# A decoder kernel with a recurrence: routing of the last stage inside the recurrence's laps, norms in two groups at three stage entries

## The reference

```
x = x + _L0_attn_ref(...)   # and L0_xattn, L0_ffn (router, top 2 of 8 experts)
x = x + _L1_attn_ref(...)   # and L1_xattn, L1_ffn: top 2 of 8 routed experts, 2 shared ones
x = x + _L2_attn_ref(...)   # and L2_xattn, L2_ffn: silu, gelu, gelu, scales
x = x + _L3_attn_ref(...)   # and L3_xattn, L3_ffn
```

```
routing = _l2norm(hs.reshape(B, S, E, D));  expr = (x @ expr_w.T).reshape(B, S, E, D)
gram = einsum('bsed,bsfd->bsef', routing, routing);  diff_n = _l2norm(gram - eye)
penalty = mean(sum(diff_n ** 2))              # one number over all 800 tokens
scores = (1 - cos(expr, routing)) * (1 + penalty)
top_v, top_i = top_k(scores, 2);  mult = softmax(top_v)
out = sum over the two chosen e of mult * mlp_e(x)  +  shared mlp(x)
```

## Time and profile before

| | |
|---|---|
| median of 3 runs | 3295.4 us (3287.6 to 3300.6) |
| profiled execution, own time | 3299.5 us |
| its span, first to last instruction | 3297.7 us |
| TensorE busy | 2989.2 us, 91% |
| VectorE busy | 1466.9 us, 44% |
| ScalarE busy | 741.6 us, 22% |
| GpSimd busy | 207.6 us, 6% |
| moved by DMA | 192.77 MB, mean 58 GB/s |

### The profile page before, as it was taken

The page is one execution under the profiler, slowest core; times in us unless marked ns, Lnnn a source line. Parts: engine busy times, 40 slices in busy tenths (PEclk is TensorE's granted clock), DMA queues, the critical chain, the costliest instruction groups (busy, mean ns, idle before and its releaser), DMA issues.

```text
span 3297.7 us, 62708 instructions
## 1 busy us (share of the span) xinstructions
PE 2989.2 (91%) x25725; PEld 1712.0 (52%) x25725; DVE 1466.9 (44%) x3548; ACT 741.6 (22%) x1835; POOL 207.6 (6%) x377
## 2 busy tenths in 40 slices
PE   6878889789988999899879879999999999999487
PEld 4554456579755555455546643444444444444277
DVE  4545335311256566200574422455555555555622
ACT  2331134211122454211014311111111111111100
POOL 2001110020210000000200000000000000000012
PEclk8889989699989999899889979999999999999799
DMA  4000000259400000410000076000000000000186
GB/s 144 1 1 1 13 9 1 108 191 331 152 27 1 1 1 1 138 51 26 1 1 1 2 203 184 13 21 17 21 21 17 21 17 21 21 17 21 37 284 204
DMA packets 79206, 192.77 MB, mean 58 GB/s; under 512 B 32664, under 2 KB 54917, under 8 KB 67366
## 3 DMA queue, kind: packets, MB, share of 16 engines
q1 hardware_dynamic: 74966, 184.17, 17.2%
q0 software_dynamic: 4096, 6.57, 0.7%
HBM read 161.29 MB, written 29.39 MB: 58 GB/s over the span
## 4 chain that ended last, share of the span: by engine, by line
PE 81%; DVE 9%; ACT 3%; issue 3%; DMA 2%; POOL 1%; SPq 1%; POOLq 0%; DVEq 0%; ACTq 0%
PE banks L1159 31%; PE banks L984 8%; PE banks L816 4%; PE banks L539 3%; PE banks L1127 3%; PE banks L710 3%; PE banks L492 3%; PE banks L1187 2%; PE banks L1048 2%; PE banks L1060 2%; PE banks L838 2%; PE banks L856 1%; PE banks L862 1%; PE banks L878 1%; PE banks L605 1%
## 5 line engine op out<-in xcount | busy, mean ns | idle before, releaser
L1159 PE MATMUL banks<-arena 128*32 128x384 f32 x12800 | 1032.2, 486 | 1.1 <-DVE arena L2089 1.1
L1159 PEld LDWEIGHTS banks<-arena 128*32 128x32 f32 x12800 | 431.9, 110 | 601.6 <-issue 599.2
L1498 ACT ACTIVATE arena<-arena 128x256 f32<-128x256 f32 x200 | 83.2, 416 | 753.9 <-DVE arena L2101 753.9
L2101 DVE TENSOR_TENSOR arena<-banks,arena 128x256 f32<-128x256 f32 x200 | 85.0, 425 | 293.2 <-PE banks L1159 293.2
L984 PE MATMUL banks<-arena 128*128 128x400 f32 x512 | 172.5, 499 | 1.5 <-DVE arena L2051 0.8
L816 PE MATMUL banks<-arena 128*100 128x256 f32 x512 | 150.7, 453 | 18.0 <-ACT arena L1423 5.4
L539 PE MATMUL banks<-XNT,arena 128*128 128x400 f32 x384 | 147.6, 526 | 8.3 <-ACT XNT L1251 3.9
L1240 ACT ACTIVATE arena<-banks 128x512 f32<-128x512 f32 (+2 forms) x120 | 68.6, 572 | 383.7 <-PE banks L1048 151.1
L710 PEld LDWEIGHTS banks<-arena 32*121 32x121 f32 x1536 | 105.9, 197 | 62.9 <-ACT arena L1342 47.3
L984 PEld LDWEIGHTS banks<-arena 128*128 128x128 f32 x512 | 97.1, 190 | 76.8 <-DVE arena L2051 1.4
L1698 DVE TENSOR_REDUCE arena<-banks 100x4 f32<-100x1444 f32 x64 | 106.3, 1661 | 65.0 <-PE banks L666 64.8
(11 more groups left out here) (314 smaller groups left out, 4098.6 us busy)
## 6 DMA issues: line engine op xcount, KB each, us to landing
arena<-fc SPq DMA_DIRECT2D x22, 1024.0 KB, 6.9
arena<-pj SPq DMA_DIRECT2D x22, 1024.0 KB, 5.2
arena<-gu SPq DMA_DIRECT2D x21, 1024.0 KB, 7.1
arena<-whh SPq DMA_DIRECT2D x32, 384.0 KB, 11.8
arena<-dn SPq DMA_DIRECT2D x21, 512.0 KB, 5.2
arena<-xw SPq DMA_DIRECT2D x408, 24.0 KB
xw<-arena SPq DMA_DIRECT2D x6, 1536.0 KB, 7.8
arena<-hh SPq DMA_DIRECT2D x16, 512.0 KB, 3.3
```

Of the source, the lines that this page charges most:

```text
L1159: last = nc.tensor.matmul(banks[32 * j:32 * j + 32, 2 * c + i, 0:384].rearrange("p (g n) -> p g n", g=3), hT[:, 1 - i, 32 * ub:32 * ub + 3 ...
L1498: nc.scalar.activation(rz[:, c, :], pre[:, c, :], ACT.Sigmoid).then_inc(sem["rz_done"], 1)
L2101: nc.vector.tensor_tensor(pre[:, c, :].rearrange("p (g n) -> p g n", g=2), banks[:, 2 * c + i, 0:2 * P].rearrange("p (g n) -> p g n", g=2) ...
```

## The change

Three things. First, at the three entries: batches 0 to 3 go through `statistics`, `norm_group` and a further `turn_group` inside the stream, three items before its end (`next_at`); at the entry VectorE norms batches 4 to 7 only (`norm_rest`) and TensorE transposes these (`turn_rest`). In A and B features of the first half of the tokens stand before `turn_rest`; in A the shared expert's weights are loaded before the stage ends, into another place, and `sort_pairs` comes after 8 of the 16 feature units as before, but with the router between them. `wih` moves to another place and is loaded during B's feed forward.

Second, the routing of the last stage: each lap ranks the tokens of the lap before it on VectorE (norms, scores without the penalty's factor, which doesn't change their order, two choices, places), TensorE adds two small matmuls per lap (`rank_lap`), and GpSimd scatters the lap's tokens with their pair number to `region_rows` (8 regions of 896 rows, filled beforehand from zeros with one transfer of 7.4 MB in B). TensorE's loop gets nine laps of ten steps written out. After the recurrence only the last lap is ranked, between the shared expert's features; the penalty is worked out between the tiles (`penalty`) and multiplies the stored top values.

Third, each tile's result is scattered from GpSimd straight to `pair_vals` by pair number, behind the landing of the previous one; half of the shared down product comes before the last tile's down product; eight plain loads replace the 16 gathers.

```diff
@@ TensorE, entries
-            turn_all()
-            pe.wait_ge(sem["l_rb"], 32)
-            router_rows(cent[:, :].rearrange("p (k e) -> p k e", k=C))
...
-            features(up_w[1], range(8))
+            features(up_w[1], range(0, 8, 2))
+            turn_rest("A")
+            pe.wait_ge(sem["l_rb"], 32)
+            router_rows(cent[:, :].rearrange("p (k e) -> p k e", k=C))
+            features(up_w[1], range(1, 8, 2))
             sort_pairs(0)
...
-            turn_all()
-            pe.wait_ge(sem["l_w2"], 48)
-            for f in range(8):
-                for half in range(2):
+            pe.wait_ge(sem["l_w2"], 32)
+            for q, (f, half) in enumerate(TWO_HALVES):
+                if q == 2:
+                    turn_rest("B")
...
@@ TensorE, recurrence
+            def rank_lap(lap, bank):
+
+                pe.wait_ge(sem["picked"], lap + 1)
+                chosen_l = work_l[:, 11, 0, :]
+                nc.tensor.matmul(banks[0:ROWS, bank, 0:E], earlier_l, chosen_l, start=True, stop=True, skip_group_check=True)
+                nc.tensor.matmul(banks[0:ROWS, bank, E:2 * E], ones[0:ROWS, 0:ROWS], chosen_l, start=True, stop=True, skip_group_check=True
+                                 ).then_inc(sem["ranked"], 1)
...
-            with pe.Fori(0, S // 2) as t:
+            with pe.Fori(0, LAP // 2) as t:
                 for i in range(2):
...
+                    step_of(i, 4 * t + 2 * i)
+            with pe.Fori(1, LAPS) as lap:
+                for k in range(LAP):
+                    step_of(k % 2, 2 * LAP * lap + 2 * k)
+                    if k == 6:
+                        rank_lap(lap, 4)
...
+                if t == 11:
+                    penalty_sum()
+                if t == PAIR_TILES:
+                    pe.wait_ge(sem["l_held"], 16)
+                    held_rows(range(4))
                 if t >= 1:
                     gated_down(t - 1, ups[t - 1])
-            pe.wait_ge(sem["l_held"], 16)
-            down(h3, held_down, 4, of=lambda b: slice(b, T, B))
+            held_rows(range(4, B))
@@ VectorE
+            def norm_rest(ph):
+
+                ready = norms_before(ph, len(KINDS[ph]), 0) + 1
+                inverse_root(rstd[:, 4:B], stats[:, 4:B, 7], rstd[:, B + 4:])
+                for b in range(4, B):
+                    last = nc.vector.tensor_scalar(XN[:, b * D:(b + 1) * D], X[:, b * D:(b + 1) * D], stats[:, b, 6:7],
...
                     if k == 0:
-                        dve.wait_ge(sem["l_expr"], 16 * lap)
+                        dve.wait_ge(sem["l_seen"], 16 * lap)
+                        dots_of(1, chunk, 0)
                     if k == 1:
...
+                        dots_of(2, chunk, 1)
+                    if k == 2:
+                        settle()
+                        norms_of(chunk)
+                    if k == 3:
+                        scores_of(chunk)
+                        dots_of(8, chunk, 0)
+                    if k == 4:
+                        top_of(chunk, 0)
+                        dots_of(7, chunk, 1)
+                    if k == 5:
+                        top_of(chunk, 1)
+                        lap_chosen()
+                        dots_of(6, chunk, 0)
+                    if k == 6:
+                        dots_of(3, chunk, 1)
+                        dots_of(9, chunk, 0)
+                    if k == 7:
+                        lap_placed(lap, 4)
+                        pair_products(3, 1)
...
+            gated_features(0)
+            settle()
+            norms_of(last_lap)
+            gated_features(1)
+            scores_of(last_lap)
...
@@ GpSimd
-            scatter(1)
-            gather(1)
+            norm_group("C", 2, 0)
+            pool.wait_ge(sem["l_fill"], 16)
+            for lap in range(1, LAPS + 1):
+                pool.wait_ge(sem["placed"], lap + 1)
+                pool.wait_ge(sem["l_src"], 32 * lap)
+                for k in range(2):
+                    nc.gpsimd.indirect_dma_start(region_rows[:, :], bass.IndirectOffsetOnAxis(ap=rows_il[:, k:k + 1], axis=0),
+                                                 row_src[:, k, :], None).then_inc(sem["l_sorted"], 16)
+            for t in range(PAIR_TILES):
+                pool.wait_ge(sem["y_ready"], PAIR_TILES + t + 1)
+                if t >= 1:
+                    pool.wait_ge(sem["l_pv%d" % ((t - 1) % 2)], rows_of(0, t - 1, 2))
+                nc.gpsimd.indirect_dma_start(pair_vals[:, :], bass.IndirectOffsetOnAxis(ap=sorted_ids[:, t % 5], axis=0),
+                                             pair_y[:, t % 2], None).then_inc(sem["l_pv%d" % (t % 2)], 16)
@@ SP
+            def load_sorted(t):
+
+                if t >= 5:
+                    sp.wait_ge(sem["xt_full"], PAIR_TILES + t - 4)
+                    sp.wait_ge(sem["l_pv%d" % ((t - 5) % 2)], rows_of(0, t - 5, 2))
...
+            load(arena[:, AT_WIH:AT_WIH + 6144], "wih", "l_gru")
             sp.wait_ge(sem["phase"], 4)
-            load(arena[:, 24576:30720], "wih", "l_gru")
...
+                    if k == 2:
+                        load_sources(bass.ds(lap - 1, 1), lap)
...
-            tile_transfers(1, PAIR_TILES - 1)
+            load_sources(slice(LAPS - 1, LAPS), LAPS)
+            region_transfers()
```

More of the change, by code:

```diff
@@ L98 @@
 PAIR_TILES = (T * 2 + E * (P - 1)) // P
+TWO_HALVES = [(0, 0), (1, 0), (0, 1), (1, 1)] + [(f, half) for f in range(2, 8) for half in range(2)]
 class Count:
@@ L1216, in _, with held_rows @@
             ups = []
+            def held_rows(batches):
+                for b in batches:
+                    tokens("d", [(h3[:, f, b:T:B], held_down[:, f, :]) for f in range(4)], D)
             for t in range(PAIR_TILES + 1):
@@ L1984, in shared_rows, with pair_tiles @@
                 own()
-            def pair_tiles(stage):
+            def pair_tiles(stage, between=lambda t: None):
                 def turned(t):
@@ new lines, in _ @@
+            scores_of(last_lap)
+            gated_features(2)
+            top_of(last_lap, 0)
+            gated_features(3)
+            top_of(last_lap, 1)
+            lap_chosen()
+            signal("scored")
+            gated_features(4)
+            lap_placed(LAPS, 2)
+            gated_features(5)
+            count, tiles, first, end = (count_l[:, k] for k in range(4))
+            step(nc.vector.scalar_tensor_tensor(count, cst("rank")[0:1, :], float(CAP), base_l[0:1], ALU.mult, ALU.add))
@@ new lines, in _ @@
+            step(nc.vector.tensor_tensor(end, first, tiles, ALU.add))
+            step(nc.vector.tensor_tensor(tiles_cl, end.unsqueeze(1).to_broadcast([1, 24, E]), tile_no_l.unsqueeze(2).to_broadcast([1, 24, E]), ALU.is_le))
+            step(nc.vector.tensor_tensor(tiles_pl, tiles_cl, tiles.unsqueeze(1).to_broadcast([1, 24, E]), ALU.mult))
+            passed, expert, region = tiles_fl[:, 0], tiles_fl[:, 1], tiles_fl[:, 2]
+            step(nc.vector.tensor_reduce(expert, tiles_cl, AX, ALU.add))
@@ L2222, in _ @@
+            pair_tiles(1, penalty)
+            shared_rows(batches=range(4, B))
             pairs_back(1, lambda g: phase_over() if g % 2 else None)
```

550 lines of the change are left out of this document (371 added, 179 removed).

## The result

The changed kernel takes 3284.97 us (median of 20 runs, 3270.15 to 3296.15), the kernel before 3294.66 (20 runs beside them, 3285.14 to 3311.42): a ratio of 0.9963, 95% interval 0.995 to 0.9976. On a second chip it was 0.9927 (0.99 to 0.9953). By these ratios the change gains 12 and 24 us; the medians differ by 10 and 20. Forecast were 44.5, and 3284.97 lies just above the range's upper end of 3284.

The account below looks back on a forecast made before the run. TensorE was taken to bound the recurrence and the last stage's tiles. Terms of -28 (entries, net), -37, -6.5, +5, +20 and +2 summed to -44.5 us, from 3295.4 to 3251; range 3222 to 3284, some 8 in 10.

Parts of the forecast that it names:

- Entry of A: At the first whole stage's entry, TensorE's 9.8 us idle and half the transposes, 2.0, go: 11.8 us less.
- Entry of B: At the second whole stage's entry, idle time and half the transposes go and the clock stays up: 14.1 us less.
- Entry of C: At the third whole stage's entry, idle shrinks from 9.8 to 5.5 us and transposes by half: 6.3 us less.
- Streams: Inside the streams, three groups of eight added transposes and 1.2 us of statistics in B's rounds: 4 us more.
- Jumps: In TensorE's ten-step recurrence loop, each of 8 jumps back waits 2.5 us for a fetch: 20 us more.
- Rival (a): In TensorE's recurrence loop, the long body costs nothing at its jumps: 3231 us; chance 0.25.
- (d): In the recurrence loop, jumps cost far more than one fetch, making the kernel slower: 3312 us and up; chance 0.06.
- Tail: From the recurrence's end to the last stage's first tile: that tile comes 37 us earlier.
- Tiles: In the last stage's tiles, stores become scatters that each wait for the previous landing: 0.1 us a tile, 2 us more.
- Rival (b): In the last stage, tile scatters become a chain, 6.5 us a tile instead of 5.5, +18: 3269 us; chance 0.12.
- End: After TensorE's last projection, plain loads and 16 additions take 12.0 us where 18.5 stood: 6.5 us less.
- rival (c): The routing slots in the recurrence's laps overflow, or the stage entries give half: 3265 to 3275 us; chance 0.12.

Follow-up runs that it names:

- the first profile: The first profiled execution of the changed kernel itself, nothing edited: a span of 3282.7 us against 3297.7 before.
- all twelve profiles after: Profiles of the changed kernel, taken twice, and of ten variants of it; no single time.
- the second run of the changed kernel: The changed kernel once more, nothing edited, on another chip: 3278.14 us, 0.9927 of the kernel before.

## Why the prediction was wrong

Every idle time that was to go went or shrank as forecast, and the loop lost about what was taken off for it. What failed were four terms of the sum: the entry of C, the tiles, the entry of A and the tail. In each, something behind the edited place set the next time: a late transfer, SP's queue, the chain of scatters, the granted clock. Against the terms:

- **Entry of A, -11.8: got -9.4 in one profile and -4 to -5.5 in eight.** The idle time went, but the stretch behind it took some back, in two ways. The prediction said that A is at half clock on either side (the granted clock before was 0.50 from 620 to 650 us) and nothing is gained by that; it took nothing as lost either. But the first features now run in that stretch. The shared expert's up products are 64 records of TensorE's; before, and in the first profile (its first 16, 8.22 us, stand further up):

```profile
652.22 12.65 PE L984 MATMUL banks<-XNT,arena 128*128 128x400 f32 x32
...
667.47 10.99 PE L984 MATMUL banks<-XNT,arena 128*128 128x400 f32 x32
```

```profile
643.11 7.84 PE L1036 MATMUL banks<-XNT,arena 128*128 128x400 f32 x16
...
653.55 12.69 PE L1036 MATMUL banks<-XNT,arena 128*128 128x400 f32 x32
```

  That is 28.8 us for 23.6, at a granted clock of 0.68 for the first 16. And in those eight profiles VectorE's addition of the shared expert's rows stands still for 8.0 to 9.4 us beside GpSimd's scatters and fills, for a cause that stays open (see the last section); TensorE waits for it 3.2 to 3.6 us in six of them, and in the other two 2.6 and 2.7 us at the same place without a cause named. In the profile before it waited 1.4 us there. The prediction saw that the first pair tile's rows are behind SP's wait and wrote "nothing for it" of the earlier sort; the loads' order was worth 6.9 us more.
- **Entry of B, -14.1: right.** From B's last projection to C's stream it was 262.2 and 262.3 us before and is 248.1 in all twelve profiles after: 14.1. The granted clock in it went from 0.97 to 1.00, as the prediction had it. Over the longer stretch of the table, by the middle of each range, it is 13.
- **Entry of C, -6.3: got +1 to +3.** This is the step that was missing. The entry itself did as forecast (5.8 us of idle time for 9.8), and the sum had no term for the stage behind it. Before, that stage moved 31 MB in 122 us, at a share of 0.88, and TensorE still hardly waited for ScalarE's copies (0.3 us); from that share I take it that the transfers had little room left. The change puts a store of 0.8 MB ahead of them and begins them 5 us later; ScalarE's waits for stores go from 14 to 43 us and TensorE's for ScalarE to 5.3 to 6.5. Together that costs 8 us, and moving the store gives it back.
- **Streams, +4: nothing to be seen.** The routing's small steps fitted their slots too: one overrun of 0.74 us in the whole recurrence.
- **Ranking matmuls, +5: 6.6** (1038.8 against 1032.2 with no gap left at a jump, the 0.74 within it).
- **Jumps, +20: 14.9 to 17.4.** Mechanism right, 1.9 to 2.2 us each for 2.5. Rival (a) is out, and (d) too.
- **Tail, -37: -29 to -32.** The expert tables were known 38.7 us after the recurrence (some 36 forecast, by the sum of the steps), and the first rows were turned 46.9 us after it (44 forecast, 81.4 before). The rest was lost behind that, 4.7 us to the first product where it was 1.2: I let all first loads start together. They start 1.1 us apart, and TensorE turns the rows of tile 1, the last but one in that row, ahead of its first product: 5.5 us, by the run that reorders them.
- **Tiles, +2: +9 to +14.** Rival (b) named the mechanism, with 18 us, and I gave it 0.12. "Start, 1 us of GpSimd, landing as late as the old stores" is what the trace shows: landings of 2.4 to 7.0 us, median 4.8, and 1 us on GpSimd, against a tile of 5.5. Their mean is 4.8 too, so with the 1 us a scatter's turn is 5.8, a little over a tile. The chain cost 7 to 12 of the rival's 18 us, by the run that takes it away, and five and two buffers don't take that up; the other 2 are there without it.
- **End, -6.5: -4 to -5.** VectorE's additions start 1.5 us behind its last one of the shared rows, not at once:

```profile
3271.16 4.16 DVE L2107 SCALAR_TENSOR_TENSOR X<-arena,small,X 100x256 f32<-100x256 f32 x9 [1.50 <-DMA arena<-pair_vals]
```

The entries together gave 15 to 21 us of the 32.2, so the half of rival (c) that has them give half, at 0.12 with its other half, came true as well.

Summed with the middle of each range: -4.5 - 13 + 2 + 6.6 + 15 - 30 + 11.5 - 5 = -17.4, between the 12 and 24 us that were timed. The 27 that are missing from 44.5 are 8 in C's stage, 9.5 in the tiles, 7 in A, 7 in the tail and 4 in smaller ones, less 4 of the streams and 5 of the jumps. These last two costs came out smaller than forecast and hid 9 us of the miss.

## What to carry to other kernels

When a wait is taken from an engine, look at the share of the DMA engines in the stage behind it. Where that is near 1, as here at 0.88, a store put ahead of its transfers and a later begin of them can cost more than the wait saved: here 8 us against 6. In SP's queue a load waited for the condition of one ahead of it: A's rows went out 0.4 us behind the down weights, and 20.8 us ahead of them once moved. So put what is needed first, first; three such reorderings gave some 20 us here by their stretches, about as much as the whole change. This loop on TensorE had no gaps with a body of 1540 instructions and eight of 2 us with 2060, and a nested loop in its body brought it there with no gap of its own.

## What the runs showed of the hardware

- A body of 1540 instructions jumped back 18 times inside and 8 times outside with no packet of the instruction queue behind its first lap. Bodies of some 2060 and 2570 were fetched anew in every lap, 10 and 12 packets of 16 KB, two more than their length, and each jump stopped TensorE for 1.5 to 2.3 us. Its granted clock was 1.00 over the recurrence of the changed kernel, with eight such gaps.
- VectorE's addition of the shared rows waited 8.04 us for something that the profile calls remote, and went on 0.2 us after GpSimd's last instruction of that run. Eleven of the twelve profiles after have such a wait, 7.3 to 9.4 us long and ending within 0.8 us of that instruction's end, in four of them some 0.7 us ahead of it. The profile before has one of 5.92 us in the same addition, ended by "remote" too, but 4.9 us ahead of GpSimd's end. Rows of VectorE and of GpSimd of the second run of the changed kernel:

```profile
685.40 0.75 DVE L2071 TENSOR_TENSOR X<-X,banks 100x256 f32<-100x256 f32 x2 [8.04 <-remote]
```

```profile
682.15 0.99 POOL L2511 DMA_INDIRECT pair_rows<-XN,arena  x1 [0.30 <-issue]
683.13 0.55 POOL L2554 MEMSET arena<- 128x512 f32 x1
...
685.06 0.10 POOL L2559 MEMSET idle_g<- 100x1 f32 x1
```

  TensorE had filled the bank by 682.3 (48 matmul records, three banks' worth, from 671.70 on in 10.60 us), so for the last 3 us of the wait at least it wasn't that. The wait spans more than six instructions of GpSimd's. In the first profile the same code had no such wait. No run takes GpSimd's work away there, and the cause stays open.
- A scatter of 128 rows of 1 KB from GpSimd landed 2.4 to 7.0 us after its issue among the loads of the tiles, with the DMA engines at a share of 0.78 (3133.8 to 3255). The changed kernel's scatters of 80 rows of 1 KB in the recurrence, at a share of 0.09, landed after 2.3 to 2.7 us.
